# Gathered values: of each root GpSimd makes the power alone, VectorE adds epsilon and makes the offset two tiles later

## The chip, the cores and the metric

The kernel runs on one core of a Trainium2 chip. The core has five engines that work side by side, each through its own instructions in order: PE (TensorE, matrix products), DVE (VectorE), ACT (ScalarE), POOL (GpSimd) and SP (SyncE, which here only starts transfers). They wait for one another through semaphores. The metric is the device time of one execution in microseconds; lower is better.

## The reference, cut to what matters

The program is eight layers in a row (four pairs of an attention layer and a feed-forward layer), each followed by a layer norm. The change lies in the seventh, which picks for each of 4 x 1024 tokens the 8 best of 4096 keys and mixes the 8 value rows that go with them:

```python
Q = jnp.einsum('bsd,bdr->bsr', x, shared_compress)
scores = jnp.einsum('bsr,nr->bsn', Q, K) / math.sqrt(K.shape[1])   # 4096 keys
topk_scores, topk_idx = jax.lax.top_k(scores, kk)                  # kk = 8
weights = jax.nn.softmax(topk_scores, axis=-1)
selected_V = V[topk_idx]
output = jnp.einsum('bskd,bsk->bsd', selected_V, weights)
...
x = _layernorm(x + output)     # (r - mean) / sqrt(var + 1e-5), per token over 128 features
```

The norm is made as r * rstd + offset with rstd = (var + eps) ** -0.5 and offset = -mean * rstd.

## The kernel before, in words

The stage is `top_keys_stage` (tiles with the prefix `tk_`). Its tokens come in 32 tiles of 128 tokens (`ALL = 32`), one token to a partition. A set-up part makes the queries; then every engine runs its own loop over the tiles, and the order of the work is simply the order in which the code of each engine stands:

- PE: 16 matmuls of tile t with the keys (L2945), then `mix(t - 6)`, eight matmuls with the identity that add up the eight weighted value rows (L2931).
- ACT: copies the scores of tile t out of PSUM in four pieces (L2619), on the way `scale(t - 6)`, which multiplies the gathered rows with their weights (L2596), and `normalise(t - 14)`, which writes y = r * rstd + offset (L2606); at the end of a tile `weigh(t - 1)` makes the softmax weights and waits for the best eight (L2585).
- DVE: `select(t)`, a MAX8 (L2746) and a FIND_INDEX8 (L2748) over 4096 scores, then `close(t - 5)`: reciprocal of the weights' sum, r (L2760), its statistics (L2763) and moments (L2764).
- POOL: `gather(t)`, eight indirect DMAs that fetch one value row per token each (L2534), and after every fourth tile `root(g)` for the group g of four tiles that was closed: in the code it stands behind gather(4g + 8).
- SP: loads the old x again and stores y, four tiles at a time (L2494, L2498); its last store ends the stage, and the next stage (`moe_`) begins behind a barrier of all engines.

`root(g)` waits for the moments of its four tiles and makes four instructions on 128x4 elements: minus_mean (L2525), plus_eps (L240), the power -0.5 (L241) and the offset (L2527). gather(t) waits for `index_ready`, and for `mixed` of tile t - 8, whose slot it fills. There are eight groups, so eight roots; root(6) and root(7) stand behind the last gather, the other six stand between gathers.

Of the kernel before, what the change touches and what calls it, by code (L numbers as in the profile page):

```python
# [13 lines left out]
ALU = mybir.AluOpType  # L14
# [3 lines left out]
P = 128  # L18
# [5 lines left out]
PER_HALF = HALF // P  # L24
LN_EPS = 1e-5
# [212 lines left out]
def rsqrt_on_pool(steps, pool, out, value, plus_eps, eps, power):  # L238

    steps.link(pool.tensor_tensor(plus_eps, value, eps, ALU.add))  # L240
    return pool.tensor_tensor(out, plus_eps, power, ALU.pow)  # L241
# [2121 lines left out]
def top_keys_stage(nc, x_in, x_out, fetched, first_x, c, next_weights, next_x):  # L2363
# [16 lines left out]
    GROUPS = B * HALVES  # L2380
# [3 lines left out]
    CLOSE_LAG = 5  # L2384
    NORM_LAG = 3 * PER_HALF + 2
    KEPT_R = 2 * PER_HALF
    SQRT_WIDTH = float(P) ** 0.5
    with ExitStack() as ctx:
        m = Room(ctx, nc, "tk")
# [3 lines left out]
        h_proj = m.sb("h_proj", [P, B])  # L2393
        keys = m.sb("keys", [P, KEYS])
        ones = m.sb("ones", [P, P])
        power = m.sb("power", [P, PER_HALF]); eps = m.sb("eps", [P, PER_HALF]); plus_eps = m.sb("plus_eps", [P, PER_HALF])
        minus_one = m.sb("minus_one", [P, PER_HALF]); minus_mean = m.sb("minus_mean", [P, PER_HALF])
        x = first_x.x; xT = m.sb("xT", [P, B, T])

        values = m.sb("values", [P, SLOTS, TOP, P])  # L2400
# [19 lines left out]
        moments = m.sb("moments", [P, KEPT_R, 2]); rstd = m.sb("rstd", [P, KEPT_R]); offset = m.sb("offset", [P, KEPT_R])  # L2420
# [21 lines left out]
        best_ready, minus_ready, index_ready, weight_ready, scaled, mixed = (  # L2442
            m.sem(n) for n in ("best_ready", "minus_ready", "index_ready", "weight_ready", "scaled", "mixed"))
        gathered = [m.sem(f"gathered{i}") for i in range(SLOTS)]
        r_ready, moments_ready, offset_ready, y_ready = (m.sem(n) for n in ("r_ready", "moments_ready", "offset_ready", "y_ready"))
        dve_steps, pool_steps = m.sem("dve_steps"), m.sem("pool_steps")
        big_loads = [(compress, c["compress"]), (keys[:], c["keys"])]

# [16 lines left out]
        def after(eng, sem, count):  # L2465

            if count > 0:
                eng.wait_ge(sem, count)
# [10 lines left out]
        def half_of(g):  # L2479
            return slice(g % HALVES * PER_HALF, (g % HALVES + 1) * PER_HALF)  # L2480
# [3 lines left out]
        @block.sync  # L2484
        def _(sp):
            for b in range(1, B):
                sp.dma_start(x_all[:, b], x_in[b]).then_inc(x_loaded[b].sem, x_loaded[b].unit)
            for dst, src in big_loads:
                sp.dma_start(dst, src).then_inc(big.sem, 16)
            next_weights.load(sp)  # L2490

            def load(g):
                sp.wait_ge(r_ready, (g + 1 - HALVES) * PER_HALF)
                sp.dma_start(x[:, half_of(g)], x_in[g // HALVES][:, half_of(g), :]).then_inc(x_again[g % HALVES], 16)  # L2494

            def store(g):
                sp.wait_ge(y_ready, (g + 1) * PER_HALF)
                sp.dma_start(x_out[g // HALVES][:, half_of(g), :], y[:, half_of(g), :]).then_inc(stored[g % HALVES], 16)  # L2498

            for g in range(HALVES, GROUPS + HALVES):  # L2500
                if g < GROUPS:
                    load(g)
                if g == GROUPS + 1:
                    for i in range(HALVES):
                        sp.wait_ge(stored[i], 16 * (B - 1))
                    sp.dma_start(next_x.x[:], x_out[0]).then_inc(next_x.arrived, 16)
                store(g - HALVES)
            for i in range(HALVES):
                sp.wait_ge(stored[i], 16 * B)

        @block.gpsimd
        def _(pool):
            steps = Steps(pool, pool_steps)
            pool.memset(ones[:], 1.0).then_inc(built, 1)
            pool.memset(power[:], -0.5).then_inc(built, 1)
            pool.memset(eps[:], LN_EPS).then_inc(built, 1)
            pool.memset(minus_one[:], -1.0).then_inc(built, 1)
            pool.wait_ge(built, 4)

            def root(g):  # L2520

                group = half_of(g)
                pool.wait_ge(moments_ready, (g + 1) * PER_HALF)
                after(pool, offset_ready, g)
                steps.do(pool.tensor_tensor(minus_mean[:], moments[:, group, 0], minus_one[:], ALU.mult))  # L2525
                steps.link(rsqrt_on_pool(steps, pool, rstd[:, group], moments[:, group, 1], plus_eps[:], eps[:], power[:]))
                pool.tensor_tensor(offset[:, group], minus_mean[:], rstd[:, group], ALU.mult).then_inc(offset_ready, 1)  # L2527

            def gather(t):
                slot = t % SLOTS  # L2530
                pool.wait_ge(index_ready, t + 1)
                after(pool, mixed, t + 1 - SLOTS)
                for k in range(TOP):
                    pool.indirect_dma_start(  # L2534
                        out=values[:, slot, k, :], out_offset=None, in_=c["values"],
                        in_offset=bass.IndirectOffsetOnAxis(ap=index[slot][:, k:k + 1], axis=0)).then_inc(gathered[slot], 16)

            for t in range(ALL + CLOSE_LAG):
                if t < ALL:
                    gather(t)  # L2540
                g, at = divmod(t - CLOSE_LAG, PER_HALF)
                if g >= 0 and at == PER_HALF - 1:
                    root(g)
# [87 lines left out]
        def _(dve):  # L2631
            steps = Steps(dve, dve_steps)
# [108 lines left out]
            def select(t):  # L2741

                slot = t % SLOTS
                dve.wait_ge(S.free.sem, scores_kept(t))
                after(dve, mixed, t + 1 - SLOTS)
                dve.max(best[:, slot, :], scores[:, t % KEPT, :]).then_inc(best_ready, 1)  # L2746
                dve.wait_ge(best_ready, t + 1)
                dve.max_index(index[slot][:], best[:, slot, :], scores[:, t % KEPT, :]).then_inc(index_ready, 1)  # L2748

            def close(t):  # L2750

                g, at = divmod(t, PER_HALF)
                own = t % KEPT_R
                if at == 0:
                    after(dve, x_again[g % HALVES], 16 * (g // HALVES))
                dve.wait_ge(mixed, t + 1)
                dve.wait_ge(weight_ready, t + 1)
                after(dve, y_ready, t + 1 - KEPT_R)
                steps.link(dve.reciprocal(inv[:, own:own + 1], total[:, t % (2 * TILES):t % (2 * TILES) + 1]))
                dve.scalar_tensor_tensor(r[:, own, :], mix_banks[t % len(mix_banks)][:, 0:P], inv[:, own:own + 1],  # L2760
                                         x[:, t % TILES, :], ALU.mult, ALU.add).then_inc(r_ready, 1)
                dve.wait_ge(r_ready, t + 1)
                steps.link(dve.bn_stats(stats[:, own, :], r[:, own, :]))  # L2763
                dve.bn_aggr(moments[:, own, :], stats[:, own, :]).then_inc(moments_ready, 1)  # L2764

            for t in range(ALL + CLOSE_LAG):
                if t < ALL:
                    select(t)
                if t >= CLOSE_LAG:
                    close(t - CLOSE_LAG)  # L2770
                if t % TILES == TILES - 1:
                    steps.restart()
            steps.restart()

        @block.tensor
        def _(pe):
# [106 lines left out]
            for b in range(B):  # L2883
                ins = pe.transpose(to_dve[0][:, b * P:(b + 1) * P], imp_wide[:, b, :], ident[:])
            ins.then_inc(chain_full, 1)
            pe.wait_ge(built, 4)
            pe.wait_ge(chain_ready, 4)
            pe.matmul(to_dve[1][:, 0:B], ones[:], imp_sum[:], start=True, stop=True).then_inc(chain_full, 1)
            for b in range(B):
# [45 lines left out]
            for t in range(ALL):  # L2935
                b, at = divmod(t, TILES)
# [651 lines left out]
```

## Time and profile before

| what | value |
|---|---|
| median of 3 runs | 2123.44 us (2122.04 to 2123.99) |
| the profiled execution, its own time | 2122.32 us |
| its span (first to last instruction) | 2120.4 us |
| busy share of the span: PE, DVE, ACT, POOL | 89%, 74%, 58%, 29% |
| mean granted clock of TensorE | 0.937 of full speed |

The profile is of one execution, taken by the hardware. It is read like this: a row of a timeline has the start in us from the span's start, the duration, the engine, the line, the operation, the tile written and the tiles read, and in brackets the idle time of the engine ahead of it and what ended that. "issue" means that nothing seen in the profile was waited for. Busy shares are averages over eight stages with different limits, so the stage at hand (about 1508 to 1977 us) is read by itself.

### The profile page before, as it was taken

The page shows a single profiled execution, that of the slowest core. Times are in us where ns is not written, and L with a number is a line of the kernel's source. Part 1 is how long each engine was busy: PE and PEld are TensorE (multiplying, and loading weights), DVE is VectorE, ACT ScalarE, POOL GpSimd, SP SyncE. Part 2 cuts the span into 40 slices and gives each one's busy share as a digit, 9 for nine tenths or more (in the row PEclk, how much of TensorE's full clock was granted, in tenths as well). Part 3 has the DMA queues.
Part 4 walks back from the last instruction along what each step waited for, and adds up shares of the span by engine and source line. Part 5 has one row for each costly group of instructions (what it writes and reads, how often), then busy time and mean ns, then how long its engine had stood idle before and what let it go on. Part 6 is the DMA issues. An engine that isn't in the chain of part 4 may idle for free. (4 is left out here: it accounts for less than half of the span.)

```text
span 2120.4 us, 31998 instructions
## 1 busy us (share of the span) xinstructions
PE 1879.8 (89%) x10615; PEld 1279.2 (60%) x10624; DVE 1569.4 (74%) x3770; ACT 1227.2 (58%) x2532; POOL 610.6 (29%) x801
## 2 busy tenths in 40 slices
PE   7999979999699999579999999999789989983797
PEld 5667644444477777458888887888664444443342
DVE  4555547677448888658999999999435999994498
ACT  3334436666255555178888887887214667673465
POOL 2221216778302121200000000000002777777122
PEclk9999989999699999789999999999779999996799
DMA  2000020000300000000000000000400122222100
GB/s 91 30 30 0 30 87 11 16 6 11 104 6 11 21 11 11 10 15 2 6 16 6 2 16 6 1 6 16 190 2 14 53 56 61 69 61 61 45 26 25
DMA packets 34695, 65.80 MB, mean 31 GB/s; under 512 B 8406, under 2 KB 19742, under 8 KB 33782
## 3 DMA queue, kind: packets, MB, share of 16 engines
q1 hardware_dynamic: 26358, 47.16, 6.5%
q0 software_dynamic: 8192, 16.79, 3.1%
q8 instruction: 80, 1.31, 0.3%
q14 instruction: 65, 0.53, 0.1%
HBM read 51.34 MB, written 12.58 MB: 30 GB/s over the span
## 5 line engine op out<-in xcount | busy, mean ns | idle before, releaser
L2183 DVE SCALAR_TENSOR_TENSOR pk_level<-pk_sums,pk_least 128x1024 f32<-128x1024 f32 x256 | 321.7, 1276 | 22.9 <-ACT pk_sums L2092 21.6
L2092 ACT ACTIVATE pk_sums<-pk_sum 128x512 f32<-128x512 f32 x512 | 278.7, 602 | 94.5 <-PE pk_sum L2302 92.1
L2534 POOL DMA_INDIRECT tk_values<-top_keys_values,tk_index x256 | 242.3, 947 | 196.4 <-DVE tk_index L2748 118.4
L2310 PE MATMUL pk_weights<-product_keys_early_ident,pk_level 128*128 128x128 f32 x2048 | 269.5, 274 | 26.3 <-DVE pk_level L2183 24.3
L2310 PEld LDWEIGHTS pk_weights<-product_keys_early_ident,pk_level 128*128 128x128 f32 x2048 | 225.9, 141 | 52.9 <-DVE pk_level L2183 33.8
L2945 PE MATMUL tk_to_act<-tk_keys,tk_xT 128*128 128x512 f32 x512 | 233.0, 602 | 23.2 <-ACT tk_scores L2619 22.1
L2945 PEld LDWEIGHTS tk_to_act<-tk_keys,tk_xT 128*128 128x128 f32 x512 | 94.1, 192 | 144.3 <-issue 92.5
L1755 PEld LDWEIGHTS er_outs<-experts_early_w,er_hT 128*128 128x128 f32 x1024 | 134.0, 192 | 59.7 <-issue 56.4
L1165 PE MATMUL ml_outs<-experts_early_we,ml_xT 128*128 128x512 f32 x320 | 161.3, 632 | 3.5 <-DVE ml_r L1022 3.5
L2302 PE MATMUL pk_sum<-pk_lay_corners,pk_partsT 96*128 96x256 bf16 x1024 | 154.2, 272 | 0.9 <-ACT pk_sums L2092 0.9
L2746 DVE MAX8 tk_best<-tk_scores 128x8 f32<-128x4096 f32 x32 | 141.1, 4409 | 15.1 <-ACT tk_scores L2619 15.1
L240 POOL TENSOR_TENSOR pk_plus_eps<-pk_moments,pk_eps 128x4 f32<-128x4 f32 x8 | 11.2, 1406 | 452.3 <-DVE pk_moments L224 452.3
L2748 DVE FIND_INDEX8 tk_index<-tk_best,tk_scores 128x8 uint32<-128x4096 f32 x32 | 141.4, 4419 | 0.0
L1022 DVE SCALAR_TENSOR_TENSOR ml_r<-ml_outs,ml_gates,ml_r 128x128 f32<-128x128 f32 x384 | 105.0, 342 | 47.7 <-PE ml_outs L1165 36.7
L1448 ACT ACTIVATE er_hT<-er_to_act,experts_early_b 128x512 f32<-128x512 f32 x128 | 85.5, 686 | 93.2 <-PE er_to_act L1744 92.3
L2619 ACT ACTIVATE tk_scores<-tk_to_act 128x1024 f32<-128x1024 f32 x128 | 126.2, 1011 | 20.4 <-PE tk_to_act L2945 20.4
L1755 PE MATMUL er_outs<-experts_early_w,er_hT 128*128 128x128 f32 x1024 | 134.5, 275 | 0.0
L1744 PE MATMUL er_to_act<-er_xT,experts_early_w 128*128 128x512 f32 x256 | 133.4, 604 | 0.0
L2073 ACT ACTIVATE pk_partsT<-pk_to_act 96x1024 bf16<-96x1024 bf16 x128 | 132.0, 1036 | 0.0
L2302 PEld LDWEIGHTS pk_sum<-pk_lay_corners,pk_partsT 96*128 96x128 bf16 x1024 | 99.6, 97 | 26.0 <-issue 15.4
L2931 PE MATMUL tk_to_dve<-tk_values,top_keys_early_ident 128*128 128x128 f32 x512 | 69.6, 295 | 38.6 <-ACT tk_values L2596 38.6
L891 ACT ACTIVATE ml_scaled<-ml_outs,ml_gates 128x128 f32<-128x128 f32 x256 | 70.1, 387 | 52.7 <-PE ml_outs L1165 51.6
(437 smaller groups left out, 3677.4 us busy)
## 6 DMA issues: line engine op xcount, KB each, us to landing
tk_scores<-top_keys_compress SPq DMA_DIRECT2D x1, 4096.0 KB
tk_values<-top_keys_values,tk_index POOLq DMA_INDIRECT x256, 2.5
att_x_proj<-x_first SPq DMA_DIRECT2D x4, 512.0 KB, 5.0
att_x_res<-x_first SPq DMA_DIRECT2D x4, 512.0 KB, 4.3
x_after_attention<-att_y SPq DMA_DIRECT2D x4, 512.0 KB, 4.9
experts_early_w<-experts_w SPq DMA_DIRECT2D x2, 1024.0 KB
x_after_attention<-ml_y SPq DMA_DIRECT2D x8, 256.0 KB, 2.0
experts_ahead_x<-x_after_attention SPq DMA_DIRECT2D x8, 256.0 KB, 3.3
```

Of the source, the lines that this page charges most:

```text
L1165: pe.matmul(outs[f % len(outs)][:], xT[:, b % 2, t * P:(t + 1) * P], we[:, n * PER_FILL:(n + 1) * PER_FILL, :].rearrange("p e d -> p (e d) ...
L1744: pe.matmul(bank[:], w1[:, n, :], xT[:, t % 2, :], start=True, stop=True).then_inc(A.full.sem, 1)
L1755: ins = pe.matmul(bank[:, s * P:(s + 1) * P], hT[:, (t * CHUNKS + n) % (LAG + 1), s * P:(s + 1) * P], w2[:, n, :], start=k == 0 and s == 0 ...
L2073: act.activation(partsT[:, t % 3, s * PER_FILL:(s + 1) * PER_FILL, :].rearrange("k n p -> k (n p)"), bank[:].bitcast(BF16)[0:STACK, 0:PER_ ...
L2092: act.activation(sums[:, n % SUMS, half * HALF:(half + 1) * HALF], bank[:], ACT.Copy).then_inc(S.free.sem, 1)
L2183: dve.scalar_tensor_tensor(level[:, n % LEVELS, :], sums[:, n % SUMS, :], least[:, t % 2, h:h + 1], sums[:, n % SUMS, :], ALU.is_ge, ALU.m ...
L2302: ins = pe.matmul(by_column[:, j], partsT[:, t % 3, h * FILLS + c, :], lay_corners[:, c], start=True, stop=True)
L2310: ins = pe.matmul(weights[:, ch * P:(ch + 1) * P], level[:, n % LEVELS, ch * P:(ch + 1) * P], ident[:], is_transpose=True, start=h == 0 an ...
L2534: pool.indirect_dma_start(out=values[:, slot, k, :], out_offset=None, in_=c["values"], in_offset=bass.IndirectOffsetOnAxis(ap=index[slot][ ...
L2746: dve.max(best[:, slot, :], scores[:, t % KEPT, :]).then_inc(best_ready, 1)
L2748: dve.max_index(index[slot][:], best[:, slot, :], scores[:, t % KEPT, :]).then_inc(index_ready, 1)
L2945: ins = pe.matmul(bank[:, half * HALF:(half + 1) * HALF], xT[:, b, at * P:(at + 1) * P], keys[:, first:first + HALF], start=True, stop=True)
```

## The change

POOL keeps of each root the power alone. DVE adds epsilon, in an instruction behind the close of a group's fourth tile (`add_eps`), and makes the offset, in an instruction behind the close of the next group's second tile (`offset_of`), with a wait for the power. The last offset is made behind the loop. `plus_eps` has a slice for each of two groups in turn; two tiles of constants go, and there are two more semaphores.

```diff
         @block.gpsimd
-            pool.memset(minus_one[:], -1.0).then_inc(built, 1)
-            pool.wait_ge(built, 4)
+            pool.wait_ge(built, 3)
 
             def root(g):
 
                 group = half_of(g)
-                pool.wait_ge(moments_ready, (g + 1) * PER_HALF)
-                after(pool, offset_ready, g)
-                steps.do(pool.tensor_tensor(minus_mean[:], moments[:, group, 0], minus_one[:], ALU.mult))
-                steps.link(rsqrt_on_pool(steps, pool, rstd[:, group], moments[:, group, 1], plus_eps[:], eps[:], power[:]))
-                pool.tensor_tensor(offset[:, group], minus_mean[:], rstd[:, group], ALU.mult).then_inc(offset_ready, 1)
+                pool.wait_ge(plus_eps_ready, g + 1)
+                pool.tensor_tensor(rstd[:, group], plus_eps[:, group], power[:], ALU.pow).then_inc(rstd_ready, 1)
...
         @block.vector
+            def add_eps(g):
+
+                group = half_of(g)
+                dve.wait_ge(moments_ready, (g + 1) * PER_HALF)
+                after(dve, rstd_ready, g - 1)
+                dve.tensor_scalar(plus_eps[:, group], moments[:, group, 1], LN_EPS, None, ALU.add).then_inc(plus_eps_ready, 1)
+
+            def offset_of(g):
+
+                group = half_of(g)
+                dve.wait_ge(rstd_ready, g + 1)
+                dve.scalar_tensor_tensor(offset[:, group], moments[:, group, 0], -1.0, rstd[:, group],
+                                         ALU.mult, ALU.mult).then_inc(offset_ready, 1)
+
             for t in range(ALL + CLOSE_LAG):
                 if t < ALL:
                     select(t)
                 if t >= CLOSE_LAG:
                     close(t - CLOSE_LAG)
+                    g, at = divmod(t - CLOSE_LAG, PER_HALF)
+                    if at == PER_HALF - 1:
+                        add_eps(g)
+                    if at == 1 and g >= 1:
+                        offset_of(g - 1)
                 if t % TILES == TILES - 1:
                     steps.restart()
+            offset_of(GROUPS - 1)
             steps.restart()
```

On POOL, between gather(8) and gather(9) and again four tiles on, the program of the change now reads (the counts behind the DMAs are those of a run of gathers):

```order
L2530 DMA tk_values<-top_keys_values,tk_index 128x128 x72
L2523 TENSOR_TENSOR tk_rstd<-tk_plus_eps,tk_power 128x4
L2530 DMA tk_values<-top_keys_values,tk_index 128x128 x32
L2523 TENSOR_TENSOR tk_rstd<-tk_plus_eps,tk_power 128x4
L2530 DMA tk_values<-top_keys_values,tk_index 128x128 x32
```

Before, four instructions stood at each of these places:

```order
L2534 DMA tk_values<-top_keys_values,tk_index 128x128 x72
L2525 TENSOR_TENSOR tk_minus_mean<-tk_moments,tk_minus_one 128x4
L240 TENSOR_TENSOR tk_plus_eps<-tk_moments,tk_eps 128x4
L241 TENSOR_TENSOR tk_rstd<-tk_plus_eps,tk_power 128x4
L2527 TENSOR_TENSOR tk_offset<-tk_minus_mean,tk_rstd 128x4
L2534 DMA tk_values<-top_keys_values,tk_index 128x128 x32
```

Three of four have left POOL's queue at each root; the 72 DMAs are gather(0) to gather(8), the 32 those of the next four tiles.

On DVE at the end of its loop in the changed program (from the end of the close of tile 29; the program before has the same closes and neither the TENSOR_SCALAR nor the two offsets):

```order
L2760 BN_AGGR tk_moments<-tk_stats 128x2
L2773 SCALAR_TENSOR_TENSOR tk_offset<-tk_moments,tk_rstd 128x4
L2755 RECIPROCAL tk_inv<-tk_total 128x1
L2756 SCALAR_TENSOR_TENSOR tk_r<-tk_to_dve,tk_inv,top_keys_ahead_x 128x128
L2759 BN_STATS tk_stats<-tk_r 128x6
L2760 BN_AGGR tk_moments<-tk_stats 128x2
L2755 RECIPROCAL tk_inv<-tk_total 128x1
L2756 SCALAR_TENSOR_TENSOR tk_r<-tk_to_dve,tk_inv,top_keys_ahead_x 128x128
L2759 BN_STATS tk_stats<-tk_r 128x6
L2760 BN_AGGR tk_moments<-tk_stats 128x2
L2767 TENSOR_SCALAR tk_plus_eps<-tk_moments 128x4
L2773 SCALAR_TENSOR_TENSOR tk_offset<-tk_moments,tk_rstd 128x4
```

The first offset is group 6's, ahead of the close of tile 30; the last two rows are group 7's epsilon and offset, behind the last close.

## Rows read from the trace of the kernel before

**Rows 1.** Busy time of the engines in 50 us of the steady part, by stretch.
```profile
1850.00:1900.00 50.00, 45.25 (x168) 24.36 (x167) 49.28 (x38) 35.37 (x82) 37.76 (x43) 1.00 0.26 71
```

**Rows 2.** The page's costliest groups: the gathers.
```profile
L2534 POOL DMA_INDIRECT tk_values<-top_keys_values,tk_index x256 | 242.3, 947 | 196.4 <-DVE tk_index L2748 118.4
```

**Rows 3.** Timeline of POOL: the first gather, and the first root between gathers.
```profile
1628.50 1.21 POOL L2534 DMA_INDIRECT tk_values<-top_keys_values,tk_index  x1 [117.44 <-DVE tk_index L2748]
...
1717.41 0.94 POOL L2534 DMA_INDIRECT tk_values<-top_keys_values,tk_index  x1 [0.30 <-issue]
1718.37 0.21 POOL L2525 TENSOR_TENSOR tk_minus_mean<-tk_moments,tk_minus_one 128x4 f32<-128x4 f32 x1
1718.53 0.21 POOL L240 TENSOR_TENSOR tk_plus_eps<-tk_moments,tk_eps 128x4 f32<-128x4 f32 x1
1718.81 1.04 POOL L241 TENSOR_TENSOR tk_rstd<-tk_plus_eps,tk_power 128x4 f32<-128x4 f32 x1
1719.94 0.20 POOL L2527 TENSOR_TENSOR tk_offset<-tk_minus_mean,tk_rstd 128x4 f32<-128x4 f32 x1
1720.65 1.03 POOL L2534 DMA_INDIRECT tk_values<-top_keys_values,tk_index  x1 [0.51 <-issue]
```

**Rows 4.** Timeline of POOL: start of the second root, and the last gather.
```profile
1760.39 0.21 POOL L2525 TENSOR_TENSOR tk_minus_mean<-tk_moments,tk_minus_one 128x4 f32<-128x4 f32 x1
...
1959.51 0.94 POOL L2534 DMA_INDIRECT tk_values<-top_keys_values,tk_index  x1 [0.30 <-issue]
```

**Rows 5.** Timeline of DVE: MAX8 of tiles 15 and 19, and the last index.
```profile
1761.45 4.41 DVE L2746 MAX8 tk_best<-tk_scores 128x8 f32<-128x4096 f32 x1
...
1800.94 4.41 DVE L2746 MAX8 tk_best<-tk_scores 128x8 f32<-128x4096 f32 x1
...
1923.75 4.42 DVE L2748 FIND_INDEX8 tk_index<-tk_best,tk_scores 128x8 uint32<-128x4096 f32 x1
```

**Rows 6.** Timeline of all engines at the stage's end.
```profile
1962.07 2.44 ACT L2596 ACTIVATE tk_values<-tk_values,tk_weight 128x128 f32<-128x128 f32 x8 [7.16 <-DMA tk_values<-top_keys_values,tk_index]
...
1968.39 0.17 DVE L2759 RECIPROCAL tk_inv<-tk_total 128x1 f32<-128x1 f32 x1 [8.90 <-PE tk_to_dve L2931]
...
1969.31 0.18 DVE L2764 BATCH_NORM_AGGREGATE tk_moments<-tk_stats 128x2 f32<-128x6 f32 x1
1969.57 0.20 POOL L2525 TENSOR_TENSOR tk_minus_mean<-tk_moments,tk_minus_one 128x4 f32<-128x4 f32 x1 [7.34 <-DVE tk_moments L2764]
...
1969.99 1.01 POOL L241 TENSOR_TENSOR tk_rstd<-tk_plus_eps,tk_power 128x4 f32<-128x4 f32 x1
...
1971.31 1.65 ACT L2606 ACTIVATE tk_y<-tk_r,tk_offset,tk_rstd 128x128 f32<-128x128 f32 x4 [4.87 <-POOL tk_offset L2527]
```

**Rows 7.** By line: DVE operations shaped like the two added (times are ns min/median/max).
```profile
L2724 DVE TENSOR_SCALAR tk_neuron_sum<-tk_neuron_sum x1: 170/170/170, 1581.4 to 1581.4; 128x4 f32<-128x4 f32 x1
...
L2174 DVE SCALAR_TENSOR_TENSOR pk_least<-pk_largest,pk_best x32: 157/163/172, 928.0 to 1482.9; 128x8 f32<-128x8 f32 x32
```

**Rows 8.** Timeline: a power on POOL and the DVE instruction that waits for it.
```profile
2114.93 1.01 POOL L241 TENSOR_TENSOR moe_rstd<-moe_plus_eps,moe_power 128x4 f32<-128x4 f32 x1
2115.97 1.11 DVE L233 TENSOR_SCALAR moe_y<-moe_r,moe_moments,moe_rstd 128x128 f32<-128x128 f32 x4 [1.40 <-POOL moe_rstd L241]
```

**Rows 9.** Timeline of DVE and POOL in the product-keys stage: epsilon on POOL beside DVE.
```profile
1009.96 1.25 DVE L2183 SCALAR_TENSOR_TENSOR pk_level<-pk_sums,pk_least 128x1024 f32<-128x1024 f32 x1
1010.12 1.75 POOL L240 TENSOR_TENSOR pk_plus_eps<-pk_moments,pk_eps 128x4 f32<-128x4 f32 x1 [40.77 <-DVE pk_moments L224]
```

**Rows 10.** PE: a pause of the steady part (timeline), and three stretches (busy, count, granted clock).
```profile
1836.52 3.70 PE L2945 MATMUL tk_to_act<-tk_keys,tk_xT 128*128 128x512 f32 x8 [0.93 <-ACT tk_scores L2619]
...
1916.00:1926.00 10.00, 0.00 (x0) 0.51 0.20 52
...
1978.00:1988.00 10.00, 9.31 (x29) 0.51 0.31 107
1988.00:1998.00 10.00, 8.27 (x31) 1.00 0.00 0
```

More of the change, by code:

```diff
@@ L2395, in top_keys_stage @@
         ones = m.sb("ones", [P, P])
-        power = m.sb("power", [P, PER_HALF]); eps = m.sb("eps", [P, PER_HALF]); plus_eps = m.sb("plus_eps", [P, PER_HALF])
-        minus_one = m.sb("minus_one", [P, PER_HALF]); minus_mean = m.sb("minus_mean", [P, PER_HALF])
+        power = m.sb("power", [P, PER_HALF]); eps = m.sb("eps", [P, 1]); plus_eps = m.sb("plus_eps", [P, KEPT_R])
         x = first_x.x; xT = m.sb("xT", [P, B, T])
@@ L2444, in top_keys_stage @@
         gathered = [m.sem(f"gathered{i}") for i in range(SLOTS)]
-        r_ready, moments_ready, offset_ready, y_ready = (m.sem(n) for n in ("r_ready", "moments_ready", "offset_ready", "y_ready"))
+        r_ready, moments_ready, plus_eps_ready, rstd_ready, offset_ready, y_ready = (
+            m.sem(n) for n in ("r_ready", "moments_ready", "plus_eps_ready", "rstd_ready", "offset_ready", "y_ready"))
         dve_steps, pool_steps = m.sem("dve_steps"), m.sem("pool_steps")
@@ L2885, in _ @@
             ins.then_inc(chain_full, 1)
-            pe.wait_ge(built, 4)
+            pe.wait_ge(built, 3)
             pe.wait_ge(chain_ready, 4)
```

## The prediction

> **What bounds the kernel now.** I read busy time by stretch first. In the steady part of the stage DVE is busy 49.28 of 50 us and POOL 37.76 [rows 1], which reads as if DVE set the pace and POOL had a quarter of its time free. It hasn't. The costliest groups say why: an indirect DMA is shown 0.947 us long, and POOL's timeline shows 0.30 us between one and the next with nothing that is waited for [rows 2, 3], so a gather of one row per token costs 1.25 us of POOL's queue, and a tile of eight 9.99 us. Against that a tile of DVE takes (1800.94 - 1761.45) / 4 = 9.87 us [rows 5].
>
> Next, is the queue ever dry? The first gather starts at 1628.50 [rows 3] and the last ends at 1959.51 + 0.94 = 1960.45 [rows 4]: 331.95 us. 256 gathers at 1.2485 are 319.6 us. A root between gathers comes on top: four tiles and a root take 1760.39 - 1718.37 = 42.02 us [rows 3, 4], of which 32 gathers are 39.95, so the root costs 2.07. Six roots stand between gathers, 12.4 us, and 319.6 + 12.4 = 332.0. The sum meets the span to 0.1 us: **POOL's queue of instructions is full from the first gather to the last**, and DVE's last index is there at 1928.17 [rows 5], 32 us before the last gather ends.
>
> The end of the stage hangs on that last gather: it lands, ACT scales it from 1962.07, PE adds it up, DVE closes tile 31 from 1968.39, POOL makes root(7) from 1969.57, ACT writes y from 1971.31 [rows 6], SP stores it and the next stage begins. So a microsecond taken from POOL's queue between gathers is a microsecond of the kernel, and root(7) stands on the path by itself.
>
> **The change part by part.** *Six roots between gathers.* At the first root the four instructions run from 1718.37 to 1719.94 + 0.20 = 1720.14, 1.77 us; the next gather starts 0.51 us behind the last of them and is 1.03 long instead of 0.94 [rows 3]. What is left is the power, 1.04 us. If it starts where minus_mean did, it ends at 1719.41: 0.73 us less a root (0.44 ahead of the power, 0.29 behind it). The restart of the gathers (0.51 and 1.03) is not touched: I take it to follow the end of the last instruction. 6 x 0.73 = **4.38 us**. The bounds: if part of the restart runs beside the offset, only the 0.44 goes, 6 x 0.44 = 2.6; if with one instruction in place of a chain the restart shrinks to the usual 0.30 and 0.94, 6 x (0.73 + 0.30) = 6.2. I take 0.73, the difference of rows that are there.
>
> *The last root.* Before, from the end of the moments (1969.31 + 0.18 = 1969.49) to ACT's start at 1971.31 are 1.82 us, with 0.08 from DVE to POOL [rows 6]. Now: epsilon on DVE, 0.04 (as from statistics to moments) and 0.17 [rows 7]; 0.08; the power 1.01; back to DVE 0.03 [rows 8]; the offset 0.16 [rows 7]; to ACT 0.04. Sum 1.53, **0.29 us less**. Bounds: nothing to -0.4, by a hop more or less.
>
> *What DVE gets.* Eight epsilons and eight offsets of 0.21 us with their gaps, 3.4 us. They are hidden: DVE's index is ahead of POOL's gather. Tile 8's gather ends at 1718.37, and by then the lead is about one tile; from then on POOL needs 41.29 us for four tiles (42.02 - 0.73) and DVE 39.49 + 0.42 = 39.91, so the lead grows.
>
> *The wait that comes in.* offset_of(g) stands on DVE in step 4g + 10 and waits for a power that POOL makes behind gather(4g + 8). POOL is late by more than those two tiles in the end. The power of root(1) is ready at 1760.39 - 0.73 + 1.04 = 1760.70, DVE comes for it at 1762.1: no wait. Root(2): ready at 1801.99, DVE comes at 1800.94 + 5 x 0.21 = 1801.99: even. For roots 3, 4 and 5 DVE waits 41.29 - 39.91 = **1.4 us each**, 4.2 in all, and the selects of later tiles queue behind it. That costs nothing either: the last index moves from 1928.17 to 1928.17 + 12 x 0.21 + 4.2 = 1934.9, and POOL wants it for the gather of tile 31 at 1950.8 - 4.4 = 1946.4. If that cover were gone, each microsecond of wait would be one of the kernel. ACT and PE, whose next tile waits for a best or a free buffer, get the same pauses. At the end offset_of(6) waits for a power behind the last gather, at 1957.1, and holds the close of tile 30 until then; the close of tile 31 is due only at 1968.39 - 4.38 = 1964.0, so that is hidden too.
>
> *One memset less, two semaphores more:* the stage's set-up on POOL is 120 us ahead of the first gather [rows 3]; nothing.
>
> *The port.* In the product-keys stage POOL's epsilon on 128x4 elements took 1.75 us instead of 0.20, while DVE had a 1.25 us instruction that reads two large tiles [rows 9]; beside MAX8 and FIND_INDEX8, with one, it took 0.21 [rows 3]. The Trainium skill (GPSIMD Engine Reference, Key points) says that GpSimd shares its SBUF interfaces with VectorE and is held up by instructions with two SBUF inputs or in a two-port mode. By that rule this change is at risk, since it gives DVE an offset with two such inputs; the trace agrees in the one stage and shows nothing of it in the other. In the sum I leave it at nothing, as the offset is 0.16 us long; its price is a rival below.
>
> Sum: -4.38 - 0.29 = -4.67 us. The profiled execution took 2122.32 (span 2120.4 and 1.9 around it), so it would take 2117.65; the median of the runs shown is 1.12 above it, and I forecast for the median 2123.44 - 4.67 = **2118.8 us**.
>
> **The rivals.** A measurement of this kernel tells 0.2%, 4.25 us, from no change; so faster means below 2119.2, slower above 2127.7.
>
> 1. *Part of the saving was never there*: the restart of the gathers began beside the offset, and only 0.44 a root goes. -2.6 - 0.3: 2120.5. For it: 0.51 before a gather against 0.30 otherwise, with nothing named that it waits for. Chance 0.20.
> 2. *The port*: each of the six powers meets a close's 0.35 us instruction, and an offset's 0.16 holds a gather. 6 x 0.51 = 3.1 given back: 2121.9. Against it: gathers keep their 1.25 us beside all that DVE does in the steady part. Chance 0.07.
> 3. *The clock of the next stage comes back sooner.* The next stage starts at 1.2 GHz, and runs 10 us at 0.51 of full speed with PE busy 9.31 of them before it is granted all [rows 10]. If it came back 7 us sooner (my bound: most of those 10), half of 7 us would be saved, 3.5: 2115.3. Since the stage now starts 4.7 us earlier against that of the chip's own rhythm, it may go either way; before was on the slow side. Chance 0.11.
> 4. *Nothing moves*, as the end hung on DVE after all, or DVE's wait runs POOL dry: 2123.4. DVE's own work would have to grow from 39.91 to over 41.29 us in four tiles. Chance 0.03.
> 5. *Slower: PE's clock falls at a wait of DVE and stays down.* PE pauses 0.93 us once a tile now [rows 10]; at the three waits this becomes 0.93 + 1.4 = 2.3 us. The clock fell behind the last scores, where PE did nothing [rows 10]. At 1.2 GHz the matmuls that fill 9.05 of 10 us [rows 1] would take 18, 8 us too long a tile. POOL's lead of some 11 us takes up the first of them; from two slow tiles on the kernel is no longer faster, and three give 24 - 11 - 4.7 = +8: 2131.8. Against it: a pause of 0.93 us never brings the clock down, 2.3 us is nearer to that than to the 10 us of idleness, and the wait undoes itself, since it only comes while POOL is over a tile behind. Chance 0.03.
>
> **How the numbers follow.** My forecast (2117.8 to 2120.2 by its own bounds) has 0.56, and lies above the 0.2% bound with a quarter of it. Faster: 0.43 of the forecast, all of rival 3, and a little of what lies between: 0.57. Slower: rival 5 and as much for what I don't see: 0.04. The rest, 0.39, is within 0.2%. The range: the low end takes half of rival 3's gain beyond the forecast and the upper bound of the saving, 2118.8 - 1.8 - 1.8 = 2115.2; the high end holds rival 1 and most of the port's price, 2121.7. Outside are rivals 4 and 5 and the outer part of 2 and 3, under 2 in 10.
>
> **What would show it.** POOL: a power alone between gathers, 1.04 us, starting 0.02 behind the gather; from one power to the next 41.3 us; the last gather's end at 1956.1. An end at 1958 speaks for rival 1, powers of 1.3 us or gathers of more than 1.25 beside DVE's new instructions for rival 2. DVE: waits for POOL's power before the offsets of groups 3, 4 and 5, some 1.4 us each, none before the first two, and one of some 10 us at group 6 that nobody feels. The chain at the end 1.5 us from the last moments to y. The granted clock 1.00 until PE's last scores; if it is 0.5 in a stretch of the steady part, rival 5 is at work. If the last gather ends 4.4 us earlier and the kernel does not, the next stage took it, and my reading of the stage's end as the kernel's is wrong.

## The result and the profile after

The change takes 2115.12 us (median of 6 runs, 2109.65 to 2118.83) against 2123.81 (6 runs, 2122.04 to 2125.06): ratio 0.9957 [0.9943, 0.9971], 8.7 us less by the medians. The forecast was 2118.8 in 2115.2 to 2121.7: the direction is right, the size about half, and the median lies just below the range. The profiled execution took 2118.83 (span 2117.0), the longest of the six. The ratios, here and below, leave out executions more than 1.5% above the fastest of their kernel, so one can differ from the ratio of the medians (for late_5 below it does most).

POOL's timeline, with the rows that answer to [rows 3, 4] (start, duration, engine, line, operation, idle time before it):

```profile
1632.61 1.21 POOL L2530 DMA_INDIRECT tk_values<-top_keys_values,tk_index  x1 [119.28 <-DVE tk_index L2744]
...
1721.68 0.95 POOL L2530 DMA_INDIRECT tk_values<-top_keys_values,tk_index  x1 [0.30 <-issue]
1722.65 1.05 POOL L2523 TENSOR_TENSOR tk_rstd<-tk_plus_eps,tk_power 128x4 f32<-128x4 f32 x1
1723.90 1.02 POOL L2530 DMA_INDIRECT tk_values<-top_keys_values,tk_index  x1 [0.19 <-issue]
...
1763.72 1.06 POOL L2523 TENSOR_TENSOR tk_rstd<-tk_plus_eps,tk_power 128x4 f32<-128x4 f32 x1
...
1958.77 0.95 POOL L2530 DMA_INDIRECT tk_values<-top_keys_values,tk_index  x1 [0.30 <-issue]
```

The power is alone and as long as before, 1.05 us. **The next gather starts 0.20 us behind it; before, it started 0.51 behind the offset** [rows 3]. From the gather ahead of a root to the gather behind it are 1723.90 - 1721.68 = 2.22 us, against 1720.65 - 1717.41 = 3.24: 1.02 less a root, not 0.73. The first gather starts 4.1 us later than before, for reasons ahead of the stage (in seven profiles of the two kernels on the usual chips it starts between 1626.9 and 1632.6); so lengths are compared, not moments. From the first gather's start to the last one's: 326.16 against 331.01, 4.85 less.

That is less than 6 x 1.02 = 6.1. The page's row of the gathers shows where 1.3 us went back:

```profile
L2530 POOL DMA_INDIRECT tk_values<-top_keys_values,tk_index x256 | 243.6, 952 | 196.3 <-DVE tk_index L2744 120.2
```

They were 242.3 us in [rows 2]. DVE's timeline, its offsets, two MAX8 of four tiles apart, and the last index, as in [rows 5]:

```profile
1766.06 0.13 DVE L2773 SCALAR_TENSOR_TENSOR tk_offset<-tk_moments,tk_rstd 128x4 f32<-128x4 f32 x1
1766.11 4.42 DVE L2742 MAX8 tk_best<-tk_scores 128x8 f32<-128x4096 f32 x1
...
1806.08 0.16 DVE L2773 SCALAR_TENSOR_TENSOR tk_offset<-tk_moments,tk_rstd 128x4 f32<-128x4 f32 x1 [0.16 <-POOL tk_rstd L2523]
1806.16 4.43 DVE L2742 MAX8 tk_best<-tk_scores 128x8 f32<-128x4096 f32 x1
...
1847.46 0.16 DVE L2773 SCALAR_TENSOR_TENSOR tk_offset<-tk_moments,tk_rstd 128x4 f32<-128x4 f32 x1 [1.59 <-POOL tk_rstd L2523]
...
1929.57 0.16 DVE L2773 SCALAR_TENSOR_TENSOR tk_offset<-tk_moments,tk_rstd 128x4 f32<-128x4 f32 x1 [1.27 <-POOL tk_rstd L2523]
...
1934.19 4.42 DVE L2744 FIND_INDEX8 tk_index<-tk_best,tk_scores 128x8 uint32<-128x4096 f32 x1
...
1960.82 0.16 DVE L2773 SCALAR_TENSOR_TENSOR tk_offset<-tk_moments,tk_rstd 128x4 f32<-128x4 f32 x1 [12.33 <-POOL tk_rstd L2523]
```

No wait at the second offset, an even meeting at the third (0.16), waits of 1.59 and 1.27 at the fourth and the sixth, and a long one nobody feels. The last index stands (1934.19 + 4.42) - 1632.61 = 306.0 us behind the first gather, 20 us ahead of the last gather. The stage's end, all engines:

```profile
1968.57 0.18 DVE L2760 BATCH_NORM_AGGREGATE tk_moments<-tk_stats 128x2 f32<-128x6 f32 x1
1968.79 0.17 DVE L2767 TENSOR_SCALAR tk_plus_eps<-tk_moments 128x4 f32<-128x4 f32 x1
1969.05 1.00 POOL L2523 TENSOR_TENSOR tk_rstd<-tk_plus_eps,tk_power 128x4 f32<-128x4 f32 x1 [8.26 <-DVE tk_plus_eps L2767]
1970.08 0.16 DVE L2773 SCALAR_TENSOR_TENSOR tk_offset<-tk_moments,tk_rstd 128x4 f32<-128x4 f32 x1 [1.12 <-POOL tk_rstd L2523]
1970.28 1.65 ACT L2602 ACTIVATE tk_y<-tk_r,tk_offset,tk_rstd 128x128 f32<-128x128 f32 x4 [4.57 <-DVE tk_offset L2773]
```

From the end of the moments (1968.75) to y are 1.53 us, to the digit what was forecast, against 1.82. Last, the stretches of [rows 1, 10] (busy time of PE, weight loads, DVE, ACT, POOL, then the granted clock):

```profile
1850.00:1900.00 50.00, 41.93 (x156) 22.47 (x155) 48.12 (x38) 34.73 (x80) 38.02 (x41) 1.00 0.24 62
...
1978.00:1988.00 10.00, 9.31 (x27) 5.19 (x25) 5.37 (x22) 2.61 (x5) 1.35 (x2) 0.50 0.28 102
1988.00:1998.00 10.00, 8.14 (x31) 2.41 (x30) 4.41 (x9) 4.72 (x8) 2.75 (x3) 0.99 0.00 0
```

The clock of the steady part is 1.00, as forecast; DVE is busy 48.12 of 50 us, where before it was 49.28, as one of its waits falls into this stretch. Three questions are left: why the gather comes sooner behind a lone power; what DVE's waits cost; and what makes the rest, as the stage's own 4.85 + 0.29 us are little more than half of 8.7.

### The profile page after: what moved, and what is told of

It is laid out like the page before. It is cut to its first block and busy times, and to the rows that moved or that the text cites. A ratio compares the mean times of both kernels' runs of the same rounds, so it can differ in the third digit from the quotient of the medians.

```text
span 2117.0 us, 31988 instructions
## 1 busy us (share of the span) xinstructions
PE 1880.1 (89%) x10615; PEld 1279.3 (60%) x10624; DVE 1572.4 (74%) x3786; ACT 1228.1 (58%) x2532; POOL 608.2 (29%) x776
## 5 line engine op out<-in xcount | busy, mean ns | idle before, releaser
L1165 PEld LDWEIGHTS ml_outs<-experts_early_we,ml_xT 128*128 128x128 f32 x320 | 59.8, 201 | 63.7 <-issue 51.9
```

What stands on the lines that cost most here:

```text
L1165: pe.matmul(outs[f % len(outs)][:], xT[:, b % 2, t * P:(t + 1) * P], we[:, n * PER_FILL:(n + 1) * PER_FILL, :].rearrange("p e d -> p (e d) ...
```

## Why the gather starts sooner

Theory S: after an instruction as short as the offset (0.20 us) the queue needs 0.51 us; after a power of 1.04 us it is ready. Theory D: the engine gets the next gather ready while the last instruction runs, unless that one is itself held by a semaphore, as the offset of before was (it waits for the power). Two kernels put a product of constants beside the power:

```diff
                 pool.tensor_tensor(rstd[:, group], plus_eps[:, group], power[:], ALU.pow).then_inc(rstd_ready, 1)
+                pool.tensor_tensor(spare[:, g], power[:], power[:], ALU.mult)     # short_last; in short_first it stands ahead of the power
```

> The change with one more instruction on GpSimd behind each power, a product of two 128x4 constants, as short as the offset was (0.20 us). Theory S (a gather starts at the later of 0.20 us behind the end and some 0.71 us behind the start of the instruction ahead of it): the gap ahead of the next gather is 0.51 us again, and the root costs 0.29 + 0.31 = 0.60 us more than in the change, 3.6 us over six roots: first to last gather 3.6 us longer. Rival (the long gap was there because the offset waited for the power, or for the semaphore it counts up): the gap stays 0.20 and only 0.29 x 6 = 1.7 us come back.

> The change with the same short instruction ahead of each power instead of behind it. Theory S: the gap behind the power stays 0.20 us and a root costs only the 0.16 to 0.20 us more that one short instruction adds ahead of another, 1.0 to 1.2 us over six roots. Rival (any second instruction makes the gather restart slowly): the gap is 0.51 and it costs as much as with the short one last, about 3 us.

They ran on a chip on which all kernels took some 2230 us (below), so the roots are read where POOL waits for no index. POOL's timeline of the short product behind the power:

```profile
1861.67 1.05 POOL L2524 TENSOR_TENSOR tk_rstd<-tk_plus_eps,tk_power 128x4 f32<-128x4 f32 x1
1862.71 0.19 POOL L2525 TENSOR_TENSOR tk_spare<-tk_power 128x4 f32<-128x4 f32 x1
1863.06 1.02 POOL L2532 DMA_INDIRECT tk_values<-top_keys_values,tk_index  x1 [0.16 <-issue]
```

A short last instruction and a gap of 0.16: **theory S falls**. Ahead of the power the product gives 0.19. The times, 2224.74 (ratio 0.9978 [0.9942, 1.0015]) and 2226.84 (0.9993 [0.9962, 1.0025]), tell nothing on that chip. The third kernel has the same product and one wait more, as before's offset had:

```diff
                 pool.tensor_tensor(rstd[:, group], plus_eps[:, group], power[:], ALU.pow).then_inc(rstd_ready, 1)
+                pool.wait_ge(rstd_ready, g + 1)
+                pool.tensor_tensor(spare[:, g], power[:], power[:], ALU.mult)
```

> The change with a wait for the power's own semaphore on GpSimd and then a short product of constants, as the offset stood before. In the last runs a short instruction without a wait behind the power left the gap at 0.16 us and cost 0.14 us a root, so what stands last is not what matters. Theory D (the engine gets its instructions ready ahead unless a wait holds them; the gather can then start 0.19 us behind the end of the last instruction but not sooner than 0.71 behind the start of one that had to wait): the gap is 0.51 us again, and the root costs 0.29 + 0.32 = 0.6 us more than in the change, 3.7 us over six roots. Rival (it was the product with the power's result that made the gather late): gap 0.16 to 0.20, 0.3 us a root, 1.8 in all.

POOL's timeline at its first root:

```profile
1718.86 1.06 POOL L2524 TENSOR_TENSOR tk_rstd<-tk_plus_eps,tk_power 128x4 f32<-128x4 f32 x1
1720.00 0.20 POOL L2526 TENSOR_TENSOR tk_spare<-tk_power 128x4 f32<-128x4 f32 x1
1720.71 1.03 POOL L2533 DMA_INDIRECT tk_values<-top_keys_values,tk_index  x1 [0.51 <-issue]
```

The 0.51 is back at all six roots, and from gather to gather across a root are 2.81 us instead of 2.21: 3.6 over six. From the first gather's start to the last one's it is 328.41 us against the change's 325.96 there, only 2.45 more, as the gathers themselves gave 1.2 back (242.3 against 243.5). The time, 2121.06 us (0.9959 [0.9945, 0.9974]), lies 3.8 above the change's 2117.24. That this is near 3.6 proves nothing: the execution profiled (2125.17) also had a next stage of 147.7 us, where the change had 140.4 (below), and the other three were not profiled. So the gather starts 0.71 us behind the start of an instruction that had to wait, and 0.16 to 0.20 behind the end of one that hadn't. Theory D fits all of it; what the engine does in those 0.7 us no profile shows.

Without the power (epsilon on DVE is stored as rstd, so the root is left out of the computation):

> Leaves the power out: VectorE adds epsilon and that stands in place of rstd, so GpSimd has nothing but gathers and the outputs' scale is another. Theory Q: between gathers another 0.96 us a root goes (2.21 - 1.25), 5.8 us over six, and at the stage's end the power's 1.0 and two hops, 1.2: where the queue is full, first to last gather 319.9 us and the time 7 us below the change's. Rival (the queue is no longer the bound once the change is made, because VectorE is at 39.9 us of 41.3): under 3 us below. Where before takes about 2230 us: nothing beyond noise.

It took 2108.47 us (0.9900 [0.9885, 0.9914]), 8.8 less than the change. POOL's first and last gather:

```profile
1630.92 1.21 POOL L2524 DMA_INDIRECT tk_values<-top_keys_values,tk_index  x1 [119.28 <-DVE tk_index L2735]
...
1950.00 0.94 POOL L2524 DMA_INDIRECT tk_values<-top_keys_values,tk_index  x1 [0.30 <-issue]
```

319.08 us from first to last start are 255 gathers of 1.25: nothing but gathers. That is 6.9 less than the change's 326.0 on this chip, and the way from the last gather's start to the next stage is 2.6 shorter (15.5 against 18.1), less 2.4 us by which its last stage was longer (below): 7.1, of the 8.8 by which the medians differ. The extra time of the gathers in the change (1.3 us in the first profile, 1.2 in again2, 0.8 in two later ones) is gone too, 242.3 us again. It is absent wherever something follows the power, and present wherever the power stands last (also in short_first, 243.1); why stays open.

## What DVE's waits cost

```diff
-                    if at == 1 and g >= 1:
+                    if at == 2 and g >= 1:
```

> The change with the offset a tile later still on VectorE, three tiles behind its group. Both: VectorE no longer waits for the powers of roots 3 and 4 and hardly for root 5 (in the first profile of the change it waited 17.6 us in 6 waits, 12.3 of them at group 6), and first to last gather stays within 1 us of the change. Theory Q: the time is the change's within 0.1%. Rival (the waits move the clock): the time is 2 to 3 us longer than the change's, where the queue is full.

2117.83 us, 0.9943 [0.9931, 0.9956], against the change in the same comparison:

> The change once more. On the chip of the last four runs every kernel took about 2230 us, the one before too, and GpSimd's queue ran dry there (in the change it waited 17 times for an index). Where the kernel before takes about 2123 us the queue is full, and I expect: first to last gather 325 to 328 us, ratio to before 0.995 to 0.998. Theory Q (the gain is GpSimd's queue, 6.1 us over six roots, 0.3 at the last, and nothing else): the median falls by 5 to 7 us. Rival (DVE's new waits move the late scores and mixes, and with them TensorE's clock, for another 2 to 3 us): it falls by 8 to 10 again. Where before takes about 2230 us: no change beyond noise, by either.

2117.24 us, 0.9943 [0.9931, 0.9955]. DVE waited for the power 3.2 us in 2 waits instead of 17.4 us in 5, and from the first gather's start to the last one's are 325.97 us against 325.96: the waits cost the queue nothing, as the prediction said, and the times differ by 0.6 us, within what such medians spread.

## Chips on which the queue runs dry

> The change itself, once more, timed in five rounds, for a second profile. In its first profile the gathers began at 1632.61 us (before: 1628.50) and the last one ended at 1959.72: 327.1 us from first to last against 331.95, with a gap of 0.20 us between the power and the next gather where before it was 0.51. Theory S (the restart of the gathers overlaps a long last instruction): the gap is 0.20 at all six roots again, and first to last gather takes 325.5 to 327.5 us. Theory P (the rest of the 8.7 us by which the median fell comes from when TensorE's clock stands at 1.2 GHz, which differs from execution to execution): the times spread again over 5 us or more, and the execution profiled has a next stage (from its first transposes to the end) of another length than the 140.0 us of the first profile, longer where the granted clock was low for longer. Rival (the gain is all in the stage): time follows the gathers alone, spread under 2 us.

> The kernel before, once more, for a second profile. All theories of the roots: first to last gather 331.95 us within 0.3, gap of 0.51 behind the offset. Theory P: the first gather does not start at 1628.50 again but some us off, and the last stage differs from 142.5 us by up to 3; the rival (the stage alone): both within 0.5 us of the first profile. Ratio to the kernel before 1.000 within 0.001.

2239.89 us, ratio 1.0038 [1.0001, 1.0074], and 1.0012 [0.9981, 1.0043] for the kernel before against itself. There the condition of the prediction is not met. The waits of POOL in the changed kernel (time, times, longest):

```profile
POOL tk_values L2530 <- DVE tk_index L2744: 241.6, 17, 120.6
```

The 120.6 are the wait for the first index; 16 more waits, 121 us, come after it; of such waits [rows 2, 3] have 1 us, 118.4 - 117.44. Once gathers run, DVE, ACT and PE all show pauses there whose cause is not in the profile. Where POOL waits for DVE, an instruction less on POOL saves nothing.

## The rest: the last stage has three lengths

The stage behind this one begins with POOL's MEMSET of moe_power. In the profile before it is there from 1977.73 to the span's end, 142.7 us; in the change's, 140.2. Profiles of all kernels show three lengths and no others: 140.2 to 140.6, 142.7 to 142.9, and 147.7 to 147.9 us. Theory P says that this hangs on the moment at which the stage begins; rival N, that it doesn't. Products of 128x128 constants delay the last root alone:

```diff
+                if g == GROUPS - 1:
+                    for i in range(5):
+                        pool.tensor_tensor(late[:, i], ones[:], ones[:], ALU.mult)
```

> The changed kernel with five products of 128x128 constants on GpSimd in the last root alone, between its wait and its power (the third root product of this size took 0.46 to 0.48 us on GpSimd in this kernel's other runs, so about 2.4 us). They move everything behind the last root by 2.4 us and nothing ahead of it. Theory P: the last stage's length hangs on the moment at which it begins, through TensorE's granted clock, which rises to 1.00 (2.4 GHz) some 9 to 12 us into the stage and, in three profiles of five, falls again to 0.50 (1.2 GHz) for stretches; lengths seen are 140.2 to 140.5, 142.7 to 142.8 and 147.7 us. It then shows another length than the change's 140.3, most likely 147.7: the time is 2.4 + 7.3 = 9.7 us above the change's 2117, about 2127 us, ratio to before about 0.999. Rival N, the stage's length hangs on nothing of this: the time is 2.4 us above the change's, 2119.5 us, ratio 0.9955, and the stage 140.3 us long.

> As the run with five products, with two: everything behind the last root moves by 0.95 us. Theory P: the stage is 140.3 or, likelier, 142.8 us long: the time is 0.95 + 2.5 = 3.4 us above the change's, about 2120.6 us, ratio 0.996. Rival N: 0.95 us above the change's, 2118.1 us, ratio 0.9948, the stage 140.3 us.

> The kernel before with three such products in its last root, about 1.4 us. Theory P: most runs of the kernel before (2126 to 2131 us on the last chip) had the stage of 147.7 us, and its stage now begins 1.4 us later, into a shorter one of 140.3: 1.4 - 7.3 = 5.9 us less time although work was added, ratio about 0.997. Rival N: 1.4 us more, ratio 1.0007.

> The kernel before, word for word, for a second profile of its last stage on an ordinary chip. Ratio 1.000. Theory P: where its runs' median lies near 2129 us its stage is 147.7 us long, where it lies near 2123 us 142.7 us; a profiled execution above 2125 us with a stage of 142.7 us speaks against the theory. Rival N: the stage is 142.7 us long in every profile of this kernel, and what differs lies elsewhere.

These fell on another 2230 us chip: 2245.13, 2238.11, 2228.25 and 2230.26 us, ratios 0.9968 [0.9928, 1.0007], 1.0013 [0.9982, 1.0044], 0.9987 [0.9968, 1.0007] and 0.9987 [0.9961, 1.0013], which decide nothing. (The medians of late_5 and late_2 lie above that of the kernel before there, 2234.22.) The products came to 0.36 us each, so the delays are 1.8, 0.7 and 1.1 us and not 2.4, 0.95 and 1.4. The lengths: 142.9, 140.4, 140.5, and **147.7 for the kernel before itself, which had shown 142.7**: the same program has more than one length, and N in its strict form falls. From here on the expectations use P for a length drawn anew in each execution, and N' for one that belongs to the kernel: before never shows 140.4, the change always does. The pairs were repeated where the kernels take their usual time:

> The changed kernel with five products in the last root, 2.4 us, again, this time beside the changed kernel on the same chip. If the stage's length is drawn anew in each execution, the median lies 2.4 us above the changed kernel's, give or take the 2 to 3 us by which medians of so few runs differ; if the stage's start fixed it, the median lies 9.7 us above. The first run of this kernel showed 142.9 us where the fixed theory said 147.7.

> The kernel before with three products in its last root, 1.4 us, again. Drawn anew: ratio 1.0007, give or take 0.0012. Fixed by the start: 5.9 us less than the kernel before, ratio 0.997, with a stage of 140.5 us as in its first run.

> The kernel before once more, for a profile of its last stage on another chip; ratio 1.000. In its four profiles so far that stage took 142.7, 142.7, and 147.7 us and, with three products put into its last root, 140.5: a stage whose length is drawn anew in each execution (theory P) shows any of 140.4, 142.8 and 147.7 us, with TensorE's granted clock rising to 1.00 at 11.5 to 12.3, 10.1 to 11.0 and 9.3 us behind the stage's start in that order. Another pairing of length and rise speaks against theory P. Rival N': the kernel before never shows 140.4 us.

> The changed kernel once more. Where the chip's own stretch of gathers is that of before (start to start 1.25 us), the gathers take 327 us from the first start to the last end, 4.8 us less than before's 332, and the time is 4.9 to 6.4 us under the kernel before from the roots alone: ratio 0.9970 to 0.9977. Rival N': the change always shows a stage of 140.2 to 140.5 us (as in its three profiles on ordinary chips, against 147.7 us in the one on the first slow chip), and the ratio is 0.994 to 0.9955. Theory P: any of the three lengths may come.

> The kernel before once more, for the length of its last stage. Drawn anew in each execution: 140.4, 142.8 or 147.7 us, so far 142.7, 142.7, 142.7 and 147.7 us (and 140.5 twice with three products in its last root). Rival N': never 140.4. Ratio 1.000.

> The changed kernel once more. From the roots alone (325.7 to 327.1 us from the first gather's start to the last's end, against 332.0) and the wait behind the last, 5.2 to 6.6 us less than before: ratio 0.9969 to 0.9975; a stage of 142.8 or 147.7 us in the profile would show that the change doesn't fix its length, one of 140.4 us, the fifth in five on ordinary chips, would speak for it, with a ratio of 0.994 to 0.996.

The last column is worked out from the granted clock of short stretches, in us behind the stage's start.

| kernel | us | ratio | last stage, us | clock rises at |
|---|---|---|---|---|
| change (again3) | 2116.34 | 0.9966 [0.9954, 0.9979] | 140.5 | 12.4 |
| change (again4) | 2117.59 | 0.9948 [0.9931, 0.9965] | 140.5 | 12.4 |
| change, 1.8 us later (late_5b) | 2119.97 | 0.9985 [0.9975, 0.9994] | 142.7 | 10.2 |
| before (before_again3) | 2123.58 | 0.9993 [0.9981, 1.0006] | 142.7 | 10.0 |
| before (before_again4) | 2125.57 | 0.9997 [0.9981, 1.0013] | 147.9 | 9.7 |
| before, 1.1 us later (before_late_3b) | 2122.45 | 0.9993 [0.9976, 1.0009] | 140.6 | 12.5 |

Three stretches of the stage in four of these, at 9 to 12, 16 to 27 and 27 to 31 us behind its start; the third number from the end is the granted clock. The kernel before in its first profile:

```profile
1986.70:1989.70 3.00, 3.00 (x6) 0.46 (x4) 1.62 (x4) 1.19 (x2) 2.10 (x3) 0.81 0.00 0
...
1993.70:2004.70 11.00, 9.91 (x51) 4.73 (x51) 7.70 (x16) 6.55 (x13) 0.00 (x0) 1.00 0.00 0
2004.70:2008.70 4.00, 4.00 (x9) 1.45 (x7) 2.74 (x9) 1.54 (x3) 0.00 (x0) 0.57 0.02 4
```

before_again4, the same kernel:

```profile
1985.20:1988.20 3.00, 3.00 (x7) 0.47 (x5) 1.62 (x4) 1.19 (x2) 2.28 (x3) 0.88 0.00 0
...
1992.20:2003.20 11.00, 10.48 (x27) 3.33 (x27) 6.68 (x13) 5.46 (x10) 0.00 (x0) 0.52 0.00 0
2003.20:2007.20 4.00, 4.00 (x17) 3.33 (x16) 0.99 (x3) 0.77 (x2) 0.00 (x0) 0.50 0.00 0
```

again4, the change:

```profile
1984.70:1987.70 3.00, 3.00 (x4) 0.50 (x2) 1.57 (x4) 0.59 (x1) 2.07 (x2) 0.50 0.00 0
...
1991.70:2002.70 11.00, 10.07 (x50) 4.71 (x49) 7.81 (x17) 6.20 (x11) 0.00 (x0) 1.00 0.00 0
2002.70:2006.70 4.00, 4.00 (x14) 1.27 (x14) 3.11 (x8) 1.90 (x4) 0.00 (x0) 1.00 0.00 0
```

late_5b, the change with its last root 1.8 us later:

```profile
1986.30:1989.30 3.00, 3.00 (x6) 0.48 (x4) 1.62 (x4) 1.19 (x2) 2.08 (x3) 0.80 0.00 0
...
1993.30:2004.30 11.00, 9.91 (x51) 4.73 (x51) 7.68 (x16) 6.54 (x13) 0.00 (x0) 1.00 0.00 0
2004.30:2008.30 4.00, 4.00 (x9) 1.50 (x7) 2.80 (x9) 1.55 (x3) 0.00 (x0) 0.57 0.00 0
```

Read down the first line of each: the later the clock rises, the shorter the stage. (Before_again4: 0.88 over three us from 9.0 on is a rise at 9.7.) Where it rises at 11.5 to 12.5 us (0.50 to 0.59 of full speed at 9 to 12 us) it stays at 2.4 GHz until the last 6 us; at 10.0 to 10.9 (0.80 and 0.81 for 10.2 and 10.1) it falls to 1.2 GHz twice more, for some 3 us each; at 9.3 to 9.7 (0.88 to 0.95) it is lost for 20 us at once. This order held in every profile. Moved by its products, the change shows the clock of the kernel before and its busy times to 0.06 us, and the kernel before the clock of the change, with busy times within 0.2.

In time: late_5b lies 3.6 us above again3, where 1.8 of delay and 2.1 of stage make 3.9, a delay alone 1.8, and the forecast for a start that fixes the length, which took 7.3 for the stage, 9.7. before_late_3b lies 1.25 us below its reference, where 1.1 - 2.1 = -1.0, but its interval holds a delay alone too. So the times decide little (3.6 is also where the length drawn anew was expected). The evidence is in the lengths: 142.9 and 142.7 us with five products in the change, 140.5 and 140.6 with three in the kernel before, each on two chips with one profile each; with two products in the change it stayed at 140.4.

The kernel before stands at an edge, with rises at 10.1 and 10.0 (142.7 us) and at 9.7 (147.9). Its single executions are spread as such an edge would have it: on the usual chips 20 of 83 took more than 2128 us, none of 6 in the first comparison, 7 of 11 in the second, and 2 of 37 and 11 of 29 in two on one chip; the others took 2117 to 2126.5. But 2128 us is no sure mark of the long stage: the execution profiled with 147.9 us took 2126.0, as its first gather came early (1626.9). Of the change's 24 there none took over 2118.83. So the length is hardly drawn freely: on these chips all four profiles of the change show the short one (again2 too, 140.4), and none of three of before. N' holds that far. On the first 2230 us chip the change had 147.7 once, and so it is no property of its code either.

## Why the prediction was right or wrong

*What bounds the kernel: right.* The queue is full, a root between gathers is worth its time, and the kernel follows. no_root shows it with 6.9 us less from gather to gather and 8.8 less in all, and linked_last from the other side, with 2.45 us more from gather to gather.

*Step "six roots between gathers": the mechanism right, the term too small.* "The restart of the gathers is not touched: I take it to follow the end of the last instruction." It was touched: 0.51 became 0.20, so a root saves 1.02 and not 0.73, 6.1 us and not 4.4. The prediction had this as its bound of 6.2 but gave no rival to it, and chose 0.73 as "the difference of rows that are there". The clue was in the same rows: the offset, last ahead of the gather, starts 0.09 us behind the end of the power that it waits for (1718.81 + 1.04 = 1719.85 against 1719.94). Against that the gathers gave 0.8 to 1.3 back, which no step had: first to last start fell by 4.85, and by 5.4 in again3 and again4.

*The last root: right,* 0.29 at y; of it 0.1 to 0.2 arrive at the next stage's start (18.2 us behind the last gather's start before, 18.04 and 18.1 now).

*DVE's work and waits: right in place and price.* Forecast: none, none, even, three of 1.4, and about 10. Measured: none, none, 0.16, 1.59, 1.15, 1.27, 12.33; three_later prices them at nothing.

*The sum: failed, by what follows the stage.* It carried the next stage over unchanged, a term of nothing, and that stage became 2.1 to 2.5 us shorter; the stage itself gave 5.0 to 5.5 us against the 4.67 of the sum. With again4 against the first profile of before: first gather +3.48 (ahead of the change), gathers -5.39, end -0.14, last stage -2.13: -4.18, and the spans are 2120.4 and 2116.2. Without what happened ahead it is -7.7, near the -8.7, -7.4 and -8.4 of three comparisons; in the change's first profile it is 4.85 + 0.2 + 2.5 = 7.5. Some 1 us of the first comparison's 8.7 is assigned to nothing. It is less than the 5.7 us by which the first gather's moment differs between executions. In the second comparison, with -12.2, the median execution of before is one of those above 2128 us. If it had the long stage, 5.2 us more, the estimate is -12.9; no profile of before was taken there. Why the clock rises at one moment and not another also stays open.

*Rival 1* (0.20) had the wrong sign: more was saved at the restart, not less. *Rival 2*, the port: powers stayed at 1.00 to 1.06. The Trainium skill's rule of the shared SBUF interfaces (GPSIMD Engine Reference, Key points) shows no effect on the powers here; the gathers' 0.8 to 1.3 us are not it as far as the runs go, as they vanish with a short product behind the power and the same DVE work. *Rival 3* (0.11) named the right stage, the right sign and 3.5 us, where 2.1 to 2.5 were measured, but for the wrong reason: the clock came back later, at 11.5 to 12.4 us instead of 10.1, and was then kept. It should have been priced with the forecast and not instead of it, and with a far greater chance. *Rival 4* is what the 2230 us chips show. *Rival 5* did not occur: the clock is 1.00 in the steady part.

## What to carry to other kernels

On a queue that is always full, price an edit from the start of the instruction ahead of it to the start of the one behind it, and look at what held the last instruction: taking away its wait also gave 0.3 us at the gather behind it. When a stage follows that begins at 1.2 GHz, its length may depend on the microsecond at which it starts (here 140.5 or 142.7 us by a shift of 1.8); before crediting or blaming an edit, compare that stage's length in both profiles and take several. An edit on the full queue of one chip can be worth nothing on another where that queue waits.

## What was not expected

A gather of 128 rows starts 0.16 to 0.20 us behind an instruction of GpSimd that was not held by a semaphore, but 0.71 us behind the start of one that was. The last stage of an unchanged program took 142.7 or 147.9 us, with rises of TensorE's clock only 0.3 to 0.4 us apart. Gathers took 0.8 to 1.3 us more in all when a power stood right ahead of a gather. And two chips ran all these kernels in some 2230 us instead of 2120, with all stages up to the first gather as long as elsewhere; the cause stays open, as does what sets the moments at which the clock changes.
